# Slot stage of a routed transformer layer: the last norm and the division of the shares change engines

## The reference, cut to what matters

```
slots = q_mu + exp(q_logsig) * noise          # noise: layernorm of x
for _ in range(3):
    prev = slots
    q = _ln(slots, lnq_g, lnq_b) @ wq + bq
    logits = einsum('bnd,bkd->bnk', k, q) / scale
    attn = softmax(logits, axis=-1) + 1e-8     # over the slots
    attn = attn / sum(attn, axis=1)            # over the context rows
    upd = einsum('bnk,bnd->bkd', attn, v)
    slots = upd @ wu + bu + prev
    h = _ln(slots, lnm_g, lnm_b) @ w1 + b1
    slots = gelu(h) @ w2 + b2 + slots
    slots = _ln(slots + x_cls, lnp_g, lnp_b)
```

## Time and profile before

| | |
|---|---|
| median of 3 runs | 1074.48 us (1073.64 to 1081.28) |
| the profiled execution, its time | 1078.0 us |
| its span | 1076.2 us |
| busy, share of the span | PE 77%, PEld 62%, DVE 56%, ACT 49%, POOL 35% |
| slot stage, from the first add of layer a's results to the last norm's `nbias` | 766.5 to 957.3 us |

### The profile page before, as it was taken

One profiled execution on the slowest core, in us unless ns is written; L12 is line 12 of the kernel. 1 busy time (PEld: TensorE's weight loads), 2 busy tenths in 40 slices (PEclk: granted clock), 3 DMA queues, 4 the chain that ended last, 5 costly groups with the idle time before them and its releaser, 6 DMA issues. The chain is left out here.

```text
span 1076.2 us, 20701 instructions
## 1 busy us (share of the span) xinstructions
PE 830.2 (77%) x6337; PEld 671.3 (62%) x6338; DVE 602.9 (56%) x1968; ACT 530.9 (49%) x1108; POOL 376.3 (35%) x542
## 2 busy tenths in 40 slices
PE   2689999999999999999976797999145555540994
PEld 2568788778887778887765565777143534340563
DVE  7545556655656656557564532333587777751333
ACT  1365666666676666676634522444145455530231
POOL 0152223233233232232211373445643434215343
PEclk9889999999999999999978898999666677765897
DMA  9970000000000000000000111111630000001113
GB/s 267 299 61 1 2 2 0 0 0 0 0 0 0 0 0 0 0 0 0 2 1 1 49 55 45 53 52 44 218 124 1 0 0 0 0 1 40 49 49 95
DMA packets 46259, 40.60 MB, mean 38 GB/s; under 512 B 11883, under 2 KB 40891, under 8 KB 45707
## 3 DMA queue, kind: packets, MB, share of 16 engines
q1 hardware_dynamic: 42731, 32.91, 12.1%
q0 software_dynamic: 3488, 7.20, 2.1%
HBM read 27.85 MB, written 12.30 MB: 37 GB/s over the span
## 5 line engine op out<-in xcount | busy, mean ns | idle before, releaser
L1709 POOL TENSOR_TENSOR sb_expd<-sb_expd,sb_rden 128x512 f32<-128x512 f32 (+1 forms) x128 | 112.5, 879 | 317.3 <-DVE sb_rden L1266 317.3
L1253 DVE TENSOR_REDUCE sb_smax<-bank 128x4 f32<-128x512 f32 (+1 forms) x128 | 74.2, 580 | 100.9 <-PE bank L508 100.9
L521 PE MATMUL bank<-sb_eye,sb_expd 128*128 128x128 f32 (+1 forms) x512 | 79.8, 279 | 11.4 <-POOL sb_expd L1709 11.2
L775 PE MATMUL bank<-sb_eye,sb_z_all 128*128 128x128 f32 x96 | 24.7, 426 | 80.3 <-ACT sb_z_all L1042 80.3
L937 ACT ACTIVATE sb_probT<-bank 128x512 f32<-128x512 f32 (+1 forms) x128 | 75.6, 592 | 21.6 <-PE bank L521 21.2
L1262 DVE TENSOR_REDUCE sb_row_sum<-sb_expd 128x4 f32<-128x512 f32 (+1 forms) x128 | 73.1, 571 | 23.1 <-ACT sb_expd L942 22.9
L942 ACT ACTIVATE sb_expd<-sb_shifted 128x512 f32<-128x512 f32 (+1 forms) x128 | 69.5, 543 | 22.6 <-DVE sb_shifted L1255 22.3
L1255 DVE TENSOR_TENSOR sb_shifted<-bank,sb_smax 128x512 f32<-128x512 f32 (+1 forms) x128 | 75.0, 586 | 4.4
L482 PE MATMUL bank<-sb_hcur,sb_watt 128*128 128x128 f32 x512 | 70.2, 283 | 9.2 <-DMA sb_watt<-att_wo 9.2
L482 PEld LDWEIGHTS bank<-sb_hcur,sb_watt 128*128 128x128 f32 x512 | 64.7, 196 | 19.2 <-DMA sb_watt<-att_wo 9.6
L533 PE MATMUL bank<-sb_probT,sb_v 128*64 128x128 f32 (+1 forms) x1024 | 71.8, 284 | 3.7 <-ACT sb_probT L937 2.3
(11 more groups left out here) (253 smaller groups left out, 2016.0 us busy)
## 6 DMA issues: line engine op xcount, KB each, us to landing
sb_watt<-att_w SPq DMA_DIRECT2D x6, 512.0 KB, 5.9
sb_gate_up<-gate_up SPq DMA_DIRECT2D x1, 2816.0 KB, 13.4
sb_gate_up<-b SPq DMA_DIRECT2D x1, 2560.0 KB, 21.3
sb_blk_x<-rows_a SPq DMA_DIRECT2D x38, 65.0 KB, 1.8
rows_a<-sb_zeros SPq DMA_DIRECT2D x1, 2432.0 KB, 29.4
...
```

The lines of the kernel that those rows point to most:

```text
L521: mm = pe.transpose(trans[u % 2][0:n, h, :], expd[:, u % 2, h, 0:n], eye[:, :])
L775: mm = pe.transpose(quads(bank[2 * g])[:, n, :], src[:, 4 * g + n, 0:D], eye[:, :])
L1253: dve.tensor_reduce(smax[:, u % 2, :], s_in, X, ALU.max).then_inc(max_done, 1)
L1709: pool.tensor_tensor(e, e, rden[:, u % 2, :].unsqueeze(2).broadcast_to([P, QH, n]), ALU.mult).then_inc(norm_done, 1)
```

## The change

**The last norm.** VectorE still takes the statistics and makes `nbias` (new `centred`). ScalarE applies it (`slot_out`, a call of `normed` into `zs`), GpSimd multiplies a group by the gain (`scaled_slots`), VectorE adds the bias to a group (`slots_in`). GpSimd also makes `s_rest` from the scaled tile, with a row that holds both biases. **The shares.** ScalarE's exponentials go to TensorE as they are. GpSimd multiplies the values by `rsum` into `vus` (`shared_values`), and the 1e-8 becomes a 78th row: `att` has 1e-8 there, `vus` the sum of the values over the context. That sum is made once: VectorE sums (`vsumT`), TensorE multiplies by `wus`, ScalarE copies, and SyncE writes it to memory and reads it back as one row, ahead of the first block loads. **Loops.** All engines have the three rounds written out. `blk_in` has one set of semaphores for both layers, and `fin_step` is gone, which costs and saves nothing.

```diff
@@ SyncE, ahead of load_blocks("a")
+            sp.wait_ge(pre_slot_done, 5 * G + 2)
+            sp.dma_start(sums, vsum[:, :]).then_inc(ld_cond, 16)
+            sp.wait_ge(ld_cond, 32)
+            sp.dma_start(vus[C:C + 1, :, :], sums.unsqueeze(0)).then_inc(ld_cond, 16)
@@ TensorE
             sh_down(G - 1)
+            pe.wait_ge(pre_dve, PRE_VSUM)
+            pe.matmul(bank[1][0:B, 0:D], vsumT[:, :], wus, start=True, stop=True).then_inc(pre_slot_full, 1)
             pe.wait_ge(sh_added, G)
+            pe.wait_ge(pre_slot_done, 5 * G + 2)
...
-                    pe.wait_ge(att_ready, it * G + g + 1)
+                    pe.wait_ge(vus_ready, it * G + g + 1)
...
-                                       att[:, b, :], vu[:, b, :], start=True, stop=True)
+                                       att[:, b, :], vus[:, b, :], start=True, stop=True)
@@ ScalarE
+            act.wait_ge(pre_slot_full, 5 * G + 2)
+            act.activation(vsum[:, 0:D], bank[1][0:B, 0:D], ACT.Copy).then_inc(pre_slot_done, 1)
...
-            with act.Fori(0, SLOT_ITERS) as it:
+            def slot_out(n, lane, src):
+                normed(lane, stats_ready, n * 2 + lane + 1, zs_ready, src=src)
+
+            slot_out(0, 0, x_sb)
+            slot_out(0, 1, x_sb)
+            for it in range(SLOT_ITERS):
                 slot_queries(it, 0)
...
                 slot_turned(it, 1)
+                slot_out(it + 1, 0, S)
                 slot_gelu(it, 1)
+                slot_out(it + 1, 1, S)
@@ VectorE
+            step(dve.tensor_reduce(vsumT[:, :], vT, X, ALU.add))
...
-            def scaled(at_, lane, src, scale, shift):
...
+            def centred(at_, lane, meanwhile=()):
+
+                deviations(at_, lane, meanwhile)
+                c = slice(tiles(lane)[0], tiles(lane)[-1] + 1)
+                dve.scalar_tensor_tensor(nbias[:, c], mv_all[:, c, 0], -1.0, rstd_all[:, c],
+                                         ALU.mult, ALU.mult).then_inc(stats_ready, 1)
+
+            def slots_in(n, lane, shift):
+
+                for g in LANES[lane]:
+                    dve.wait_ge(zg_ready, n * G + g + 1)
+                    dve.tensor_tensor(group(S, g), group(zs, g), shift.unsqueeze(1).broadcast_to([P, 4, D]),
+                                      ALU.add).then_inc(S_ready, 1)
...
-                        ins = dve.tensor_scalar(att[:, b, :], att[:, b, :], rsum[0:C, b:b + 1], 1e-8, ALU.mult, ALU.add)
...
-                queries(at_, it, 1, shares(at_, it, 0))
+                slots_in(it, 1, shift)
+                queries(at_, it, 1)
+                shares(it, 0)
...
-                mlp_out(at_, 0)
+                centred(at_, 0)
+                slots_in(it + 1, 0, R["lnp_b"])
...
-                mlp_out(at_, 1)
+                centred(at_, 1)
@@ GpSimd
+            pool.memset(att_or_sent[2 * 32:P, 0:B * P], 1e-8).then_inc(sent_ready, 1)
...
+            def scaled_slots(n, lane, scale, rest, kept=True):
+                for g in LANES[lane]:
+                    pool.wait_ge(zs_ready, n * G + g + 1)
+                    pool.tensor_tensor(group(zs, g), group(zs, g), scale...., ALU.mult).then_inc(zg_ready, 1)
+                if kept:
+                    for g in LANES[lane]:
+                        pool.wait_ge(zg_ready, n * G + g + 1)
+                        pool.tensor_tensor(group(s_rest, g), group(zs, g), rest...., ALU.add).then_inc(S_rest, 1)
+
+            def shared_values(it, lane):
+                for g in LANES[lane]:
+                    pool.wait_ge(rsum_ready, it * G + g + 1)
+                    pool.tensor_tensor(vus[0:C, 4 * g:4 * g + 4, :], vu..., rsum..., ALU.mult).then_inc(vus_ready, 1)
...
                 root(n + 1, 1)
+                shared_values(it, 0)
                 keep_mid(it, 0)
                 root(n + 2, 0)
+                shared_values(it, 1)
                 keep_mid(it, 1)
                 root(n + 3, 1)
                 root(n + 4, 0)
-                if not last:
-                    keep_slots(it + 1, 0)
+                scaled_slots(it + 1, 0, R["lnp_g"], rest_b, not last)
                 root(n + 5, 0)
                 root(n + 6, 1)
-                if not last:
-                    keep_slots(it + 1, 1)
+                scaled_slots(it + 1, 1, R["lnp_g"], rest_b, not last)
```

More of the change, by code:

```diff
@@ L233, in program @@
         es_b = sb("es_b", P, D)
+        vus = sb("vus", C + 1, B, D + 1)
+        vsumT = sb("vsumT", P, B)
+        vsum = sb("vsum", B, D + 1)
         picked = sb("picked", P, B, 2, D)
@@ L342, in program @@
         normed_by_dve = sem("normed_by_dve")
+        stats_ready, zs_ready, zg_ready = (sem("sl_" + n) for n in ("stats_ready", "zs_ready", "zg_ready"))
         x3_ready, z3T_done, z3T_ready, lgb_done = (
             sem(n) for n in ("x3_ready", "z3T_done", "z3T_ready", "lgb_done"))
-        fin_step = sem("fin_step")
         x2_by_pool = sem("x2_by_pool")
@@ L1594, in slot_round @@
                 maxima(at_, it, 1)
-                for _ in shares(at_, it, 1):
-                    pass
+                shares(it, 1)
                 updates(at_, it, 1)
                 mlp_in(at_, it, 1, mlp_sums(at_, it, 0))
-                mlp_out(at_, 0)
+                centred(at_, 0)
+                slots_in(it + 1, 0, R["lnp_b"])
                 if last:
@@ L1834, in slot_round @@
                 root(n + 4, 0)
-                if not last:
-                    keep_slots(it + 1, 0)
+                scaled_slots(it + 1, 0, R["lnp_g"], rest_b, not last)
                 root(n + 5, 0)
                 root(n + 6, 1)
-                if not last:
-                    keep_slots(it + 1, 1)
+                scaled_slots(it + 1, 1, R["lnp_g"], rest_b, not last)
             root(1, 0)
-            keep_slots(0, 0)
-            root(2, 0)
-            root(3, 1)
-            keep_slots(0, 1)
-            with pool.Fori(0, SLOT_ITERS - 1) as it:
-                slot_round(it, False)
-            slot_round(SLOT_ITERS - 1, True)
+            root(2, 1)
+            pool.tensor_tensor(rest_b, R["bu"], R["lnp_b"], ALU.add)
+            pool.tensor_tensor(rest_mu, R["bu"], R["q_mu"], ALU.add).then_inc(sent_ready, 1)
+            pool.wait_ge(sent_ready, 7)
+            pool.wait_ge(exp_out["a"], 2)
+            scaled_slots(0, 0, es_b[:, :], rest_mu)
+            root(3, 0)
+            scaled_slots(0, 1, es_b[:, :], rest_mu)
+            for it in range(SLOT_ITERS):
+                slot_round(it, it == SLOT_ITERS - 1)
             root(3 + 6 * SLOT_ITERS + 1, 1)
```

90 lines of the change are left out of this document (41 added, 49 removed).

## The result

The changed kernel takes **1125.9 us** (median of 4 runs, 1124.9 to 1127.2), the kernel before 1076.7 (median of 4, 1073.6 to 1081.3): a ratio of 1.045 [1.041, 1.050]. Forecast were 1123, from 1108 to 1137. The profiled execution took 1126.2 with a span of 1123.9, 47.7 more than the 1076.2 of before.

What follows compares the result with a forecast made beforehand. No engine is full in the slot stage; a chain of marks around each round sets its time. Leg terms from +1.7 ahead of layer a to -0.6 for loops sum to +48, on 1074.5: 1123 us, range 1108 to 1137.

Steps and rivals of the forecast that it cites:

- Ahead of layer a: Before the first block loads: SyncE first needs a small matmul, copy, transfer of `sums` and second issue; +1.7, ends +0.5 and +3.
- Query bias to last maximum: Lane 0's leg: ScalarE puts lane 1's last norm ahead of lane 0's query norm; +5.3 in rounds two and three, none in round one.
- the blocking: Shared ports, VectorE and GpSimd: a VectorE operation that comes while GpSimd works waits for that instruction's end, about 1.1.
- a rule against that: Whichever engine starts first holds the shared ports: group 1's gain starts 0.5 later in four places, sum 2 more.
- Scaling the values: GpSimd, between last maximum and lane 0's update: taken as like a 128x512 add, 1.3, from 1.0 to 1.6.
- VectorE's own part in the leg 879.34 to 892.64 is what the change takes out: Lane 1's net bias to the next query bias, 13.3 before: the change removes VectorE's work there; leg forecast at +5.5, twice.
- VectorE's load: Rival, slot rounds: VectorE's load is what counts, every round loses 11.2, time 1041, faster; chance 3%.
- Gains and waits cancel: Rival, slot rounds: the 11.2 a round return as shorter legs and pay two thirds of the waits; 1074 to 1080; 2%.
- half: Rival, slot stage: the marks hold but some waits overlap; 25 to 37 more, about 1105; chance 5%.
- The clock: Rival, rounds and tail: TensorE's clock falls, logits and updates lose about 4 a round; 1136 to 1142; 8%.
- The logits' leg: Lane 0's query bias to last maximum: forecast +5.3 in rounds two and three.
- the hop alone was to cost 0.45: Update of lane 1: GpSimd's 1.3 and a hop replace four L1536 of 0.87; +0.45 a round, 1.4 in all.

Runs made afterwards that it cites:

- thinned kernels: Kernel before with VectorE's last norm applied to one tile in four only, in lane 1, lane 0 or both: 1.0002, 1.0022, 0.9988 of the kernel before.
- thinned lane 0: Kernel before with VectorE's last norm applied to one tile in four of lane 0's tiles only: 1.0022 of the kernel before.
- moved adds: Kernel before with loops written out and GpSimd's adds of lane 0's s_rest moved behind the next root: 0.9998 of the kernel before.
- the loops: Kernel before with the slot stage's loops written out on all engines, nothing else: 0.9981 of the kernel before, -2.1 us.
- reordered kernel: Changed kernel with work in another order on ScalarE, VectorE and GpSimd, s_rest adds behind the roots: 1.032 of the kernel before, stage 219.6.

## Why the prediction was right

**The method** held: the new chain was counted forward from mark to mark, and by rounds, as in the table, all legs but two are within about 0.5. The sum came to 48, the two executions differ by 48. That it is so close is luck: the two legs that are off, by -1.3 and +1.5, cancel.

**Where it erred, and what covered for it.**

- *Ahead of layer a, +1.7:* +0.4, just under my lower end of 0.5. `sums` goes out at 653.16, the row at 654.52, the first block load at 654.79, 0.74 later than before. The small matmul and the copy took the 0.7 that I had, but `sums` landed 1.4 after its issue instead of 1.8, and the second issue took 0.3 instead of 0.65. SyncE's timeline:

```profile
653.16 0.34 SPq L420 DMA_DIRECT2D sums<-sb_vsum  x1
654.52 0.22 SPq L422 DMA_DIRECT2D sb_vus<-sums  x1
```

  Half of the 0.7 is gone by the stage's start. On the chips with the pause of the last section TensorE stands 3.1 longer at this step, my upper end.

- *Query bias to last maximum, round one, 0:* +1.5. The norms are done, as I said, but the query bias itself, 0.17 long elsewhere, came beside a gain of GpSimd and took 1.11; ScalarE started 0.9 later for it. The other 0.5 lies behind ScalarE's start. The 1.11 is the blocking of the earlier trace rows in a place where I had not looked for it. VectorE's timeline of the stage's start:

```profile
782.48 3.41 DVE L1541 TENSOR_TENSOR sb_S<-sb_z_all,sb_rows 128x512 f32<-128x512 f32 x2 [1.77 <-POOL sb_z_all L1846]
...
790.55 1.11 DVE L1528 SCALAR_TENSOR_TENSOR sb_nbias<-sb_mv_all,sb_rstd_all 128x8 f32<-128x8 f32 x1 [1.87 <-POOL sb_rstd_all L1840]
```

- *The blocking goes both ways.* I took it as one-sided and gave a rule against that beside the sum, with 2 us more for it. The gain of group 1 takes 1.59 instead of 1.27, the adds behind it 2.93 instead of 2.50, and at the start VectorE's and GpSimd's pairs both take 3.4. The Trainium skill (SBUF — State Buffer, Who interferes with whom) says that the one that starts first keeps the shared ports for its whole instruction; the trace agrees in direction. The size is 0.3 in each of the places where I had 0.5, so in four places the sum needed about 1 more, not 2.
- *Scaling the values, 1.3:* 1.04. It took the 0.3 back.
- *"VectorE's own part in the leg 879.34 to 892.64 is what the change takes out":* read as a saving, this is wrong. The thinned kernels show that lane 1's net sets that leg as much as VectorE does. It did no harm to the sum, which counted the new chain and took nothing off for work removed, but it made me expect 7 us of the thinned lane 0, which gave none. For the moved adds it would have given 2, on top of the loops; they gave none either.

**The rivals.** *VectorE's load* is out three times over: leaving out 24 of the last norm's 32 operations made no round shorter, the shares taken off it cost 4.5 in the stage alone, and in the changed kernel putting them back gained 10. *Gains and waits cancel* and *half*: no leg got shorter but one, by 0.6 in all, and the waits did not overlap. *The clock:* the granted clock did fall with the longer rounds, 0.65 against 0.72 and 0.75. It cost far less than I priced it. The logits' leg, where I had put it, is no longer than its hops. What may be seen of it is in lane 1's update, at the lower level all through; that leg grew by 0.5 to 0.8 a round where the hop alone was to cost 0.45. *The order* is the cause of part: 18 of 47, by the reordered kernel with its moved adds. The other 29 I put down to the hops: ScalarE's norm of 3.2, GpSimd's gain, a bias add, and the shares' scaling behind the root, one after the other on the lane that the round waits for. Of these the gain was taken out of the changed kernel by itself (13.5) and the shares' part was run by itself (2.3 in each lane 0 leg); for ScalarE's norm and the bias add it is the count of the legs that says so.

**Left open.** Why norm and shares together cost 4.5 more in the stage than each alone is not settled: 3.6 of it lie in lane 1's update, where the granted clock is lower than with either part alone, but no run varied TensorE's clock by itself.
